# First stage of a conv and mixture-of-experts chain: shared conv in other banks, another step order, routing logits from centred weights

## What is computed

```
x = x + conv0(ln_channels(x))       # 16 images, 128 channels, 32x32
t = tokens(x); t = t + ffn0(ln(t))  # 16384 tokens, 8 experts, top 2, gated, hidden 341
x = x + conv1(ln_channels(x))       # depthwise 3x3, taps computed from the pooled image
t = tokens(x); t = t + ffn1(ln(t))  # 8 experts, top 1 with a capacity, hidden 512
```

## Time and profile before

| | |
|---|---|
| median of 3 runs | 2041.85 us (2039.49 to 2042.02) |
| profiled execution | 2049.27 us, span of its instructions 2047.5 us |
| busy, PE / PEld / DVE / ACT / POOL | 1725.7 / 962.7 / 1474.9 / 1029.6 / 1055.8 us |
| mean granted TensorE clock | 0.925 of 2.4 GHz |
| stage A (first turn of an image to first matmul of FFN tile 0) | 62.6 to 763.3 us |

### The profile page before, as it was taken

One profiled execution on the slowest core, in us unless ns is written; L12 is line 12 of the kernel. 1 busy time (PEld: TensorE's weight loads), 2 busy tenths in 40 slices (PEclk: granted clock), 3 DMA queues, 4 the chain that ended last, 5 costly groups with the idle time before them and its releaser, 6 DMA issues.

```text
span 2047.5 us, 40915 instructions
## 1 busy us (share of the span) xinstructions
PE 1725.7 (84%) x9314; PEld 962.7 (47%) x9315; DVE 1474.9 (72%) x5423; ACT 1029.6 (50%) x1740; POOL 1055.8 (52%) x1198
## 2 busy tenths in 40 slices
PE   2679889988988849999999995589898959999957
PEld 2334444444444424555555552355555534444447
DVE  5777677776767656777777774777777657888857
ACT  1444344434434426777777773245656525555524
POOL 1003445435544646777777776435666444666620
PEclk8689999998999969999999998689989979999979
DMA  8600111111111124222222221312221013222146
GB/s 265 174 11 31 45 36 42 40 42 40 44 34 35 38 64 114 80 82 75 82 81 77 82 67 49 103 34 82 72 63 44 26 48 111 78 80 79 35 116 213
DMA packets 180063, 149.06 MB, mean 73 GB/s; under 512 B 19302, under 2 KB 161822, under 8 KB 179960
## 3 DMA queue, kind: packets, MB, share of 16 engines
q1 hardware_dynamic: 153336, 98.05, 17.5%
q0 software_dynamic: 26624, 49.93, 7.2%
HBM read 76.00 MB, written 77.34 MB: 75 GB/s over the span
## 4 chain that ended last, share of the span: by engine, by line
PE 54%; DVE 16%; issue 11%; ACT 9%; DMA 4%; POOL 3%; ACTq 1%; SPq 1%; DVEq 0%; POOLq 0%
PE banks L759 12%; PE banks L760 12%; PE banks L761 12%; PE banks L754 9%; PE banks L975 5%; ACT work L1091 4%; POOL slot_rows L626 2%; ACT work L1190 2%; PE banks L772 1%; DMA slot_rows<-work,small 1%; PE banks L985 1%; DVE small L1471 1%; DMA wb_h<-ffn_rows 1%; DVE small L1496 1%; DVE small L1467 1%
## 5 line engine op out<-in xcount | busy, mean ns | idle before, releaser
L647 POOL DMA_INDIRECT ffn_rows<-work x448 | 486.1, 1085 | 238.8 <-issue 170.0
L626 POOL DMA_INDIRECT slot_rows<-work,small x384 | 389.6, 1015 | 327.3 <-DVE small L1668 146.8
L754 PE MATMUL banks<-small,work 128*128 128x128 f32 x1344 | 197.3, 285 | 179.3 <-ACT work L1091 153.2
L754 PEld LDWEIGHTS banks<-small,work 128*128 128x128 f32 x1344 | 159.7, 146 | 251.4 <-issue 142.3
L1891 DVE TENSOR_TENSOR work<-work 128x512 f16<-128x512 f32 x376 | 260.8, 694 | 12.6
L759 PE MATMUL banks<-work,wb_h 128*128 128x512 f16 x648 | 247.4, 382 | 6.1 <-issue 4.5
L761 PE MATMUL banks<-work,wb_l 128*128 128x512 f16 x648 | 247.3, 382 | 0.0
L760 PE MATMUL banks<-work,wb_h 128*128 128x512 f16 x648 | 247.2, 382 | 0.0
L759 PE MATMUL banks<-work,wa_h 128*128 128x512 f16 x576 | 235.1, 408 | 3.6 <-ACT work L1122 3.2
L1907 DVE SCALAR_TENSOR_TENSOR work<-banks,small,work 128x512 f32<-128x512 f32 x216 | 161.4, 747 | 102.9 <-ACT work L1204 102.3
L760 PE MATMUL banks<-work,wa_h 128*128 128x512 f16 x576 | 234.5, 407 | 0.0
(11 more groups left out here) (323 smaller groups left out, 3203.2 us busy)
## 6 DMA issues: line engine op xcount, KB each, us to landing
wa_l<-slot_rows SPq DMA_DIRECT2D x112, 264.0 KB, 2.9
work<-ffn_rows SPq DMA_DIRECT2D x32, 512.0 KB, 5.3
work<-in_x SPq DMA_DIRECT2D x16, 512.0 KB, 3.4
ffn_rows<-small SPq DMA_DIRECT2D x32, 256.0 KB, 3.8
out_image<-work SPq DMA_DIRECT2D x16, 512.0 KB, 3.1
ffn_rows<-work POOLq DMA_INDIRECT x448, 2.2
slot_rows<-work,small POOLq DMA_INDIRECT x384, 2.3
slot_rows<-small SPq DMA_DIRECT2D x17, 264.0 KB, 4.2
```

What stands on the lines that cost most here:

```text
L626: pool_e.indirect_dma_start(slots, bass.IndirectOffsetOnAxis(ap=slot_i[:, row_buffer(p, i, k), tt:tt + 1], axis=0), rows[row_buffer(p, i, ...
L647: pool_e.indirect_dma_start(dst, bass.IndirectOffsetOnAxis(ap=idg[old.v][:, qq, 0:1].bitcast(I32), axis=0), yt[old.u][:, qq, :], None, bou ...
L754: last = pe.transpose(dst[:, tt * P:(tt + 1) * P], x, ident)
```

## The change

- `home(j)`: the shared conv of nxt is written in `tp`, the turned image's banks, and no more in `pair[1]`. It is issued ahead of the second router matmul, and its statistics move from DVE's last weave into the weave of `group_affine(i, 1)`.
- The routing logits of old are matmuls of `acc[old]` itself with router weights from which their mean over the channels was taken in setup; DVE multiplies the products by the row's 1/std. `route_turn` and the copy of the turned rows are gone for stage A. The logits follow the turn of `acc[old]` on PE.
- Choice of experts for tokens: both choices and the mask from the shifted logits in `route_choose`, in the last weave of the step; the exponentials (one wider ACTIVATE that includes the second choice's) after the choice. `route_rest` becomes a shorter `route_place`, woven behind the statistics with `accumulate(old, 2)`.
- Image gates: ranks by comparison of all pairs of logits instead of two passes of `top`.
- PE begins a step with two taps of expert one, ACT does `route_rows` at the end of its step, and `sweep` has `peeled=2`: steps -1 to 3 written out, five passes.
- Second FFN's weights: maxima in steps -1 and 0, scales in 0, high halves on ACT at the ends of steps 1 and 2, low halves on DVE at the ends of steps 1, 2 and 3.

```diff
-STEPS_A, STEPS_C = 212, 60
+STEPS_A, STEPS_C = 184, 60
-    for t in range(first, per):
+    for t in range(first, per * peeled):
...
-    with eng.Fori(1, n // per - 1) as q:
+    with eng.Fori(peeled, n // per - 1) as q:
...
+        def home(j):
+
+            return tp if j == 0 else pair[of(j)]
...
+            def a_logits(i):
                 if some(i.b):
-                    pe.wait_ge(sem(p + "slots_known"), i.b)
+                    pe.wait_ge(sem("A_pos_read"), i.b)
                 for tt in range(TPI):
-                    last = pe.matmul(sm_b[:, tt * E:(tt + 1) * E], nT[:, tt * P:(tt + 1) * P], w, start=True, stop=True)
+                    last = pe.matmul(sm_b[:, tt * E:(tt + 1) * E], acc[i.u][:, tt * P:(tt + 1) * P], rw_centred, start=True, stop=True)
...
@@ TensorE a_step @@
-                if live(nxt, IMAGES):
-                    pe.wait_ge(sem(f"x_loaded{nxt.u}"), nxt.h * 16 + 16)
-                    turn(tp, [xcm[nxt.u][:, tt * P:(tt + 1) * P] for tt in range(TPI)]).then_inc(sem("A_xt_done"), 1)
...
-                    pe.wait_ge(sem("A_silu0"), i.b + 1)
-                    conv_half(i, 1, 0, regs, range(3))
+                    if some(i.b):
+                        pe.wait_ge(sem("A_silu1"), i.b)
+                    conv_half(i, 1, 0, regs, range(2))
+                if live(nxt, IMAGES):
+                    pe.wait_ge(sem(f"x_loaded{nxt.u}"), nxt.h * 16 + 16)
+                    if some(nxt.b):
+                        pe.wait_ge(sem("A_silu0"), nxt.b)
+                    turn(tp, [xcm[nxt.u][:, tt * P:(tt + 1) * P] for tt in range(TPI)]).then_inc(sem("A_xt_done"), 1)
+                if live(i, IMAGES):
+                    conv_half(i, 1, 0, regs, range(2, 4))
                 if live(old, IMAGES):
                     group_mean(old, 2)
...
                     turn(tp, [acc[old.u][:, tt * P:(tt + 1) * P] for tt in range(TPI)]).then_inc(sem("A_tok_done"), 1)
+                    a_logits(old)
...
                     group_mean(i, 1)
-                    conv_half(i, 2, 0, regs, range(5, 8))
+                if isinstance(i.b, int) and i.b == 0:
+                    spread_scales(2)
+                if live(i, IMAGES):
+                    conv_half(i, 2, 0, regs, range(5, 7))
                 if live(nxt, IMAGES):
+                    pe.wait_ge(sem("A_padl_done"), nxt.b + 1)
+                    conv_half(nxt, 0, 0, regs)
+                    conv_half(nxt, 0, 1, regs).then_inc(sem("A_conv_done0"), 1)
                     pe.wait_ge(sem("A_hb"), nxt.b + 1)
...
-                    conv_half(i, 2, 0, regs, range(8, TAPS))
-                    conv_half(i, 2, 1, regs, range(1))
-                if live(old, IMAGES):
-                    pe.wait_ge(sem("A_padl_done"), upto(old.b + 3, IMAGES))
-                    route_turn("A_", old)
...
-                    conv_half(i, 2, 1, regs, range(1, 4))
+                    conv_half(i, 2, 0, regs, range(7, TAPS))
+                    conv_half(i, 2, 1, regs, range(4))
                 if live(nxt, IMAGES):
                     group_mean(nxt, 0)
-                if live(old, IMAGES):
-                    logits("A_", old, vec("rw0", 0, E))
@@ ScalarE a_step, from h8 on @@
-                if live(old, IMAGES):
-                    route_rows("A_", old)
-                if isinstance(i.b, int) and i.b == 0:
-                    direct_high(range(4))
                 if live(i, IMAGES):
                     a_silu(i, 1)
...
-                if live(old, IMAGES):
-                    route_copy("A_", old)
-                if live(old, IMAGES):
-                    route_exp("A_", old)
                 if live(nxt, IMAGES):
                     a_silu(nxt, 0)
                 if live(old, IMAGES):
+                    route_rows("A_", old)
+                    route_exp("A_", old)
...
                     act.activation(rows[1][:, :, 0:C], rows[0][:, :, 0:C], ACT.Copy).then_inc(sem("A_rows2_ready"), 1)
                 if isinstance(i.b, int) and i.b == 0:
+                    act.wait_ge(sem("parked"), 16)
+                if isinstance(i.b, int) and i.b == 1:
+                    direct_high(range(4))
+                if isinstance(i.b, int) and i.b == 2:
                     direct_high(range(4, 8))
@@ VectorE a_step @@
                 weave(has_old and group_affine(old, 2),
-                      has_nxt and token_stats(lambda tt: tp_tok[:, tt, :], 1e-6, image_stats, sem("A_image_stats")),
-                      isinstance(i.b, int) and i.b == 0 and late_maxima(),
-                      has_older and route_rest(older))
-                weave(has_old and accumulate(old, 2, 0))
+                      has_nxt and token_stats(lambda tt: tp_tok[:, tt, :], 1e-6, image_stats, sem("A_image_stats")))
+                if isinstance(i.b, int) and i.b == -1:
+                    weave(late_maxima(range(5)))
+                if isinstance(i.b, int) and i.b == 0:
+                    weave(late_maxima(range(5, 8)))
+                    late_largest()
+                weave(has_old and accumulate(old, 2, 5),
+                      has_older and route_place(older))
...
-                weave(has and group_affine(i, 1))
+                if isinstance(i.b, int) and i.b == 0:
+                    power_steps(2)
+                weave(has and group_affine(i, 1),
+                      has_nxt and group_stats(nxt, 0))
+                if isinstance(i.b, int) and i.b == 0:
+                    late_scales()
                 weave(has_nxt and a_gates(nxt),
+                      has_nxt and shared_affine(nxt, 2),
                       has and accumulate(i, 1, 2),
-                      has_nxt and shared_job(nxt, 3),
-                      has_old and route_choose("A_", old, 2, 11))
+                      has_old and route_choose(old, 9))
+                if isinstance(i.b, int) and i.b in (1, 2, 3):
+                    weave(direct_low(range(3 * i.b - 3, min(3 * i.b, 8))))
```

More of the change, by code:

```diff
@@ L97, in upto, with sweep @@
     return min(value, last) if isinstance(value, int) else value
-def sweep(eng, n, step, line=None, count=0, per=2, first=-1, behind=2):
-    for t in range(first, per):
+def sweep(eng, n, step, line=None, count=0, per=2, first=-1, behind=2, peeled=1):
+    for t in range(first, per * peeled):
         step(Img(t // per, t % per, per))
@@ L114, in sweep @@
     if line:
-        line.leave(n // per - 2)
+        line.leave(n // per - 1 - peeled)
     for t in range(n - per, n + behind):
@@ L204, in build @@
         wd1_h, wd1_l, wd2_h, wd2_l = (wd_all[:, k * E * HID1:(k + 1) * E * HID1] for k in range(4))
-        work = sb("work", [P, 11800])
-        small = sb("small", [P, 2860])
+        work = sb("work", [P, 11700])
+        small = sb("small", [P, 2960])
         def carve(tensor):
@@ L280, in build @@
         both_eps = t([2 * TPI])
-        shifted, exped, probs, tmp8, place = (t([TPI, E]) for _ in range(5))
+        shift_all, exp_all = t([TPI * (E + 1)]), t([TPI * (E + 1)])
+        shifted, exped = (x[:, 0:TPI * E].rearrange("p (t e) -> p t e", e=E) for x in (shift_all, exp_all))
+        second, second_exp = (x[:, TPI * E:] for x in (shift_all, exp_all))
+        probs, tmp8, place = (t([TPI, E]) for _ in range(3))
         hots, prod2 = t([2, TPI, E]), t([2, TPI, E])
@@ L834, in a_step @@
                 if live(i, IMAGES):
[L835 removed]
+                    conv_half(i, 1, 0, regs, range(4, TAPS))
                 if live(older, IMAGES):
@@ L1066, in vectors @@
                 act.activation(vecs, sm_a[:, 0:VEC["end"]], ACT.Copy)
+                act.activation(rw_centred, sm_a[:, 136:136 + E], ACT.Copy)
                 act.activation(w2r[0:8, :], sm_a[0:8, 128:128 + EC], ACT.Copy).then_inc(sem("vecs_ready"), 1)
@@ L1121, in a_silu @@
                 par = of(j)
-                act.activation(act_o[par], pair[par], ACT.Silu, scale=gsb[:, par, 0:1], bias=gsb[:, par, 1:2]).then_inc(sem(f"A_silu{j}"), 1)
+                act.activation(act_o[par], home(j), ACT.Silu, scale=gsb[:, par, 0:1], bias=gsb[:, par, 1:2]).then_inc(sem(f"A_silu{j}"), 1)
             def a_step(i):
@@ L1313, in step, with power_steps @@
                 dve.wait_ge(sem("dve_steps"), L.step())
-            def power_scales(r):
-                first, n, done, turned = rounds[r]
+            def power_steps(r):
+                _, n, _, turned = rounds[r]
                 dve.wait_ge(sem("pe_turned"), turned + 1)
@@ L1334, in power_scales, with power_read @@
                 dve.tensor_scalar(spread[0:n, n:2 * n], ident[0:n, 0:n], si, None, ALU.mult).then_inc(sem("scale_steps"), 1)
+            def power_read(r):
+                first, n, done, turned = rounds[r]
                 dve.wait_ge(sem("pe_turned"), turned + 2)
@@ L1667, in route_place @@
-                first = 0 if choices == 2 else i.u
-                dve.tensor_copy(slot_i[:, first:first + choices, :], slot_f[:, 0:choices, :]).then_inc(sem(p + "slots_known"), 1)
```

(9 more changed lines are left out.)

311 lines of the change are left out of this document (154 added, 157 removed).

## The result

The change makes the kernel slower: 2049.2 us median (2037.6 to 2054.9 in 20 runs) against 2041.74 us (2033.0 to 2048.5 in 20 runs) of the kernel before beside it, a ratio of 1.0031 with a 95% interval of 1.0017 to 1.0045. The forecast was 2027, faster; the range, 2004 to 2048, just misses the result.

The account below looks back on a forecast made before the run. Latency between engines was taken to bound the kernel, no engine being saturated. Fourteen steps +7, head -11 and tail -10.7 sum to -14.7 us: 2034.6 against the profiled 2049.3, 2027 from the median 2041.85; range 2004 to 2048.

Parts of the forecast that it names:

- stretch 4: Loop step from the shared conv's end to the next mean read: 14.1 us, with eight rounds of `route_choose` at 2.0.
- Cost nothing: Two extra table loads at the end of ACT's step: ACT ready 1 us before the next SiLU, no cost.
- The rival with a drain of 1.38: Table switches with a drain make ACT late for the second expert's SiLU, 1.8 us a step: 2052 us, chance 0.03.
- Stretches 1 to 3: Loop step from the mean read to the shared conv's end, at full clock: 8.8, 5.4 and 7.4 us.
- stretches 2 and 3: From the turn of acc to the end of expert one, 5.4 us, then to the shared conv's end, 7.4.
- stretch 3: End of expert one to the shared conv's end, 7.4 us; DVE's affine queues behind the conv, 1.8 later than before.
- The clock: PE's half clock costs 1.2 us a step, bounds 0 and 2.4; 16.8 over the fourteen steps.
- the clock rival: The clock stays up through PE's short waits, so the 16.8 us go: 2010 us, chance 0.18.
- the slower one: Two slow clock windows fall into PE's own stretches each step, 31 us in all: 2058 us, chance 0.12.
- Peeling and the second FFN's weights: Added to the fourteen steps: 20 us for late pass starts, 23 for low halves in steps 1 to 3.
- late starts: DVE starting late where a loop pass begins: four times, 3.1 + 0.9 each, plus clock, 20 us in all.
- Head and tail: Before the fourteen steps' first mean read, -11 us; from their last to FFN tile 0, -10.7, bounds -5 and -14.

Follow-up runs that it names:

- Experiment 1: Changed kernel with POOL's addition for the next image waiting for DVE's mask of the old image: 2036.89 us, ratio 0.9965 to the kernel before.
- Experiment 2: Changed kernel with an unused one-column SiLU at the end of ACT's step, loading the table early: 2042.27 us, ratio 0.9993 to the kernel before.
- experiment 6: Changed kernel with only the shared conv's statistics put behind the affine of expert one: 2032.5 us, ratio 0.9956 to the kernel before.
- experiments 7 to 9: Unread matmuls where PE waits: changed kernel, ratio 0.9959; changed kernel plus addition, table-load, low-half and affine edits, 0.9739; kernel before, 0.9975.

## Why the prediction was wrong

The sign is wrong. The largest of the errors, 25.9 us, is larger than the whole distance from the forecast to the result, and comes from one term.

**The step that failed is stretch 4**, "eight rounds of `route_choose` alone 2.0". I priced the rounds by rows of a DVE that POOL leaves alone, and wrote of POOL only its scatters. POOL's addition after the shared conv's SiLU was in my reading of the kernel and in no term. The rounds take 3.9 (458.04 to 461.9): +25.9 over fourteen steps. Experiment 1 shows the cause of the long instruction: with the addition elsewhere it takes 0.224 us, every time. What it costs the kernel follows from the timeline; taking it away brought 13 us in the medians, since the addition then holds another instruction in part, and half clock costs more in the shorter steps. A hint was there, `L1686` at 0.58, a row of before that the prediction left out. The Trainium skill's rule on the shared ports ("SBUF — State Buffer", section "SBUF: two separate sides"), told above, was the one to weigh here, and I did not look for a POOL operation that the change moves in time without editing it.

**ACT, "Cost nothing"**: right inside a step, wrong where a pass begins. I checked that ACT has time for two more table loads, not where the second of them is issued: 6.5 us. Experiment 2 shows it. The size of a load, 1.28 and no drain, held in every switch of after. The rival with a drain of 1.38 (the Trainium skill, "ScalarE: Activation LUTs", section "What ACT_TABLE_LOAD costs") did not come: a load starts 0.02 us behind the activation ahead of it (unless it waits), and the next can start 0.01 us behind the load.

**Stretches 1 to 3** were right. Normalising ends 8.8 to 9.1 after the mean read (predicted 8.8; 10.6 with the table load on the path), stretches 2 and 3 together take 12.8 (12.8), DVE waits 1.5 for the shared conv (1.5). Some 7 us of small rounds came on top. I had seen the in-order wait in stretch 3, and called it 1.8 later; experiment 6 measures what going round it gives, 1.0 a step.

**The clock**: 15 us in place of 16.8, so neither the clock rival (2010) nor the slower one (2058) came. The 15 is a remainder, and the late statistics bear it out with 14. That it came close is in part luck: in the shorter steps of experiment 1 the statistics are 29 us late. And experiments 7 to 9 show that this term could be had back, which no case of mine had.

**Peeling and the second FFN's weights**: low halves 16.7 for 23, late starts 15 for 20. The mechanism was right (DVE idle 3.9 and 2.7 for ACT's high half at the ends of steps 1 and 2, where I had written 5 to 6), both sizes somewhat high.

**Head and tail**: -14.3 for -11, outside its bounds of -7 and -13, and -8.1 for -10.7. FFN tile 0 starts 65.2 behind the last of the fifteen mean reads, 2.6 later than forecast; the last image's mean is read 30.0 behind that (predicted 27), and tile 0 comes 35.2 later (34.6). What takes the 3 us in step 15 stays open.

Sum of the errors: steps +25.8 (25.9 + 7 + 6.5 - 6.3 - 5 - 1.8, within 0.5), head -3.3, tail +2.6: 25.1. The forecast of -14.7 becomes +10.4, which is what stage A shows in the profiles (10.5); the medians show +7.5. That the result misses the range by only 1 us is luck: errors of +42 (the held instruction, rounds, table load, tail) stand against -16 (low halves, late starts, clock, head). The range reached to 2048 on bounds of the costs I had named, and the missing one was larger than any of them.

## What to carry to other kernels

When an edit moves work on one engine, list what it thereby moves in time on the others. Here the 2.35 us addition on GpSimd cost nothing beside VectorE's reads of PSUM and 1.85 us a step beside a small operation with two SBUF inputs on the critical path. Ask of each table load, low-priority copy or first statistic which wait it is issued behind, not only whether its engine has time. And where PE waits a microsecond or two before a stretch of its own, look at the granted clock behind the wait, and try a few matmuls with unread results there: they gave 0.25% to 1.3% here, and experiment 1 shows that without them part of a saving on DVE can go to half clock.
